# An octonion FFN and autocorrelation kernel: in the third hidden chunk of a group, the up unit is placed ahead of the down unit

## The reference, cut to what matters

```python
def _L0_ffn_ref(x, w_gate, w_up, w_down):
    ...
    xp = x.reshape(B, T, 8, D // 8)
    gate = oct_ternary_linear(xp, w_gate).reshape(B, T, -1)
    up = oct_ternary_linear(xp, w_up).reshape(B, T, -1)
    h = jax.nn.silu(gate) * up
    hp = h.reshape(B, T, 8, h.shape[-1] // 8)
    out = oct_ternary_linear(hp, w_down).reshape(B, T, D)
    return out

x = L0_attn_x
xn = _layernorm(x, axis=-1)
x = x + _L0_attn_ref(xn) + _L0_ffn_ref(xn, L0_ffn_w_gate, L0_ffn_w_up, L0_ffn_w_down)
```

## Time and profile before

| | |
|---|---|
| time, median of 3 runs | 612.71 us (612.17 to 613.39) |
| the profiled execution: time | 611.43 us |
| the profiled execution: span of its instructions | 609.6 us |
| TensorE busy | 575.1 us, 94% |
| VectorE busy | 506.1 us, 83% |
| GpSimd busy | 463.1 us, 76% |
| ScalarE busy | 356.4 us, 58% |
| granted TensorE clock, mean | 0.998 of full speed |

### The profile page before, as it was taken

One profiled execution on the slowest core, in us unless ns is written; L12 is line 12 of the kernel. 1 busy time (PEld: TensorE's weight loads), 2 busy tenths in 40 slices (PEclk: granted clock), 3 DMA queues, 4 the chain that ended last, 5 costly groups with the idle time before them and its releaser, 6 DMA issues.

```text
span 609.6 us, 16256 instructions
## 1 busy us (share of the span) xinstructions
PE 575.1 (94%) x6672; PEld 533.8 (88%) x6672; DVE 506.1 (83%) x1227; ACT 356.4 (58%) x499; POOL 463.1 (76%) x362
## 2 busy tenths in 40 slices
PE   0998999989999999999999999999999999999996
PEld 0898998878989999899989998899989998999896
DVE  1875799769899889989898989989888989967854
ACT  4767885755556645865567645774476545543540
POOL 2403919999778986999769977999779977987920
PEclk9999999999999999999999999999999999999999
DMA  9520003001030022101030013002030012002011
GB/s 226 135 72 1 1 1 140 2 1 57 16 139 2 2 72 65 76 2 70 2 140 1 9 65 126 15 2 71 2 139 1 35 38 70 2 2 70 2 71 70
DMA packets 10235, 30.65 MB, mean 50 GB/s; under 512 B 913, under 2 KB 4017, under 8 KB 10161
## 3 DMA queue, kind: packets, MB, share of 16 engines
q1 hardware_dynamic: 9200, 28.22, 13.9%
q10 hardware_dynamic: 960, 1.40, 1.0%
HBM read 21.23 MB, written 8.39 MB: 49 GB/s over the span
## 4 chain that ended last, share of the span: by engine, by line
POOL 53%; issue 30%; PE 12%; DVE 1%; DMA 1%; ACT 1%; POOLq 0%; SPq 0%; ACTq 0%
POOL hop L1299 15%; POOL hs L1293 10%; POOL hs L1294 10%; POOL hs L1289 9%; POOL hs L1288 6%; PE acc L462 5%; PE acc L393 4%; DMA xr<-in_x 1%; PE acc L372 1%; POOL r L1247 1%; POOL hop L1296 1%; PE acc L439 1%; PE acc L404 0%; PE acc L365 0%; ACT junk L584 0%
## 5 line engine op out<-in xcount | busy, mean ns | idle before, releaser
L462 PE MATMUL acc<-wd,hop 114*128 114x128 f16 (+1 forms) x2944 | 169.7, 219 | 1.0 <-POOL hop L1299 0.7
L462 PEld LDWEIGHTS acc<-wd,hop 114*128 114x128 f16 (+1 forms) x2944 | 166.6, 98 | 2.3 <-POOL hop L1299 0.9
L664 ACT ACTIVATE pk<-acc 114x512 f32<-114x512 f32 (+1 forms) x120 | 70.6, 589 | 70.4 <-PE acc L462 34.0
L1288 POOL TENSOR_TENSOR hs<-hx 114x512 f32<-114x512 f32 x47 | 60.3, 1283 | 66.8 <-DVE hx L1058 59.0
L1299 POOL TENSOR_TENSOR hop<-hs,hop 114x1024 f16<-114x1024 f32 x46 | 98.2, 2136 | 7.9 <-ACT hop L719 7.9
L1296 POOL TENSOR_TENSOR hop<-hx,hop 114x1024 f16<-114x1024 f32 x46 | 98.4, 2138 | 0.6 <-ACT hop L708 0.6
L372 PE MATMUL acc<-xop,wg 128*128 128x256 f16 x704 | 84.1, 273 | 4.5 <-DVE acc L1009 4.4
L708 ACT ACTIVATE hop<-hx 114x1024 f16<-114x1024 f32 x46 | 48.6, 1057 | 65.4 <-DVE hx L1058 65.4
L365 PE MATMUL acc<-xop,wg 128*128 128x256 f16 x704 | 84.2, 273 | 1.2 <-DVE hx L1058 1.1
L372 PE MATMUL acc<-xop,wu 128*128 128x256 f16 x704 | 84.1, 273 | 0.7
L365 PE MATMUL acc<-xop,wu 128*128 128x256 f16 x704 | 84.1, 273 | 0.7 <-DVE hx L1058 0.7
(11 more groups left out here) (156 smaller groups left out, 913.3 us busy)
## 6 DMA issues: line engine op xcount, KB each, us to landing
xr<-in_x SPq DMA_DIRECT2D x16, 512.0 KB, 4.6
zx<-in_x SPq DMA_DIRECT2D x16, 512.0 KB, 3.6
out_y<-zx SPq DMA_DIRECT2D x16, 512.0 KB, 3.0
hop<-in_w_down SPq DMA_DIRECT2D x1, 1364.0 KB, 19.1
hop<-in_w_gate ACTq DMA_DIRECT2D x1, 1152.0 KB
hop<-in_w_up SPq DMA_DIRECT2D x1, 1152.0 KB
hop<-in_w_gate ACTq DMA_DIRECT2D x1, 192.0 KB
hop<-in_w_up SPq DMA_DIRECT2D x1, 192.0 KB
```

Source lines behind the costliest of these rows:

```text
L462: last = nc.tensor.matmul(acc[:, bank[n], s // 2, at:at + P], operand(g, c, t, form, level), wd[0:WIDE[c], slot, c, :], start=which == 0 a ...
L664: nc.scalar.activation(pk[0:rows, q % 2, :, :], pair[:, :, T:2 * T], ACT.Copy, scale=XS if u[0] == "X" else 1.0).then_inc(copied, 1)
L1288: nc.gpsimd.tensor_tensor(hs[:, 4:8:2, :], h[:, 0:4:2, :], h[:, 1:4:2, :], ALU.add)
```

## The change

In groups 1 to 6 the unit N(g-1,1) moves from ahead of U(g,2,0) to behind it. On VectorE the output of an N unit moves behind the second sums when the step's own unit is a G (which is now so for N1, whose output falls into the step of G21, and for N(6,0) in the last group), and `x_sums_low` of X1 moves from the end of the step of G21 to the start of the step of U21. On ScalarE the rounding of the sums of U(g,1,0) stays in the step of N1 (`late` is 6), the rounding of U20 stays in the step of U21 (+4); the rounding of the sums of U20 is still six places behind its unit, which now is the step of G00 and was that of U00. The halves of `hop` are handed out as before (`written`).

```diff
@@ the order of the units
-            if c == 1 or c == 2 and g < G - 1:
-                units += [("N", g - 1, c - 1)]
+            if c == 1:
+                units += [("N", g - 1, 0)]
             units += [("U", g, c, 0)]
+            if c == 2 and g < G - 1:
+                units += [("N", g - 1, 1)]
@@ the halves of hop
-    for u in units:
+
+    def written(u):
+        return place[u] + (1.5 if u[0] == "U" and u[2:] == (2, 0) else 0)
+
+    for u in sorted((u for u in units if u[0] in "UN"), key=written):
@@ ScalarE's roundings
-            late = 6 if g == 0 or c == 2 else 4 if (c, Y, g) == (1, 0, G - 1) else 5
+            late = 6 if g == 0 or c == 2 else 4 if (c, Y, g) == (1, 0, G - 1) else 5 + (c == 1 and Y == 0)
             if (g, c) == (G - 1, NC - 1):
                 late = 4 + 3 * (1 - Y)
-            high_at[place[u] + 3] = u
+            high_at[place[u] + (4 if (c, Y) == (2, 0) and 1 <= g < G - 1 else 3)] = u
             round_at[place[u] + late] = u
@@ VectorE, one step
+                if n - 1 in x_sums and x_sums[n - 1][2] == 1:
+                    x_sums_low(x_sums[n - 1])
                 if u in quad_no:
                     first_adds(n, u)
...
-                if n >= OPEN + 2:
-                    v = units[n - 2]
-                    if v[0] == "N":
...
+                v = units[n - 2] if n >= OPEN + 2 else ("",)
+                if v[0] == "N" and kind == "G":
+
+                    second_adds(n, u)
+                if v[0] == "N":
...
-                if u in sums_no:
+                if u in sums_no and not (v[0] == "N" and kind == "G"):
                     second_adds(n, u)
...
-                if n in x_sums:
+                if n in x_sums and x_sums[n][2] == 0:
                     x_sums_low(x_sums[n])
```

More of the change, by code:

```diff
@@ L1137, in _ @@
                         split_last(v)
-                if n >= OPEN + 2:
-                    v = units[n - 2]
-                    if v[0] == "N":
[L1141 to L1150, removed]
-                if u in sums_no:
+                v = units[n - 2] if n >= OPEN + 2 else ("",)
+                if v[0] == "N" and kind == "G":
+                    second_adds(n, u)
+                if v[0] == "N":
+                    _, g, t = v
+                    pair = bank_pair(n - 2).rearrange("p b e -> p (b e)")
+                    res = zx[:, t, :]
+                    most = D - DB
+                    dve.wait_ge(term_mm, prod_no[v] + 1)
+                    dve.wait_ge(z_done, n_no[v] + 1)
+                    nc.vector.scalar_tensor_tensor(res[:, 0:most], pair[:, 0:most], osc[:, :], res[:, 0:most], ALU.mult, ALU.add)
+                    nc.vector.scalar_tensor_tensor(res[:, most:D], pair[:, most:D], nosc[:, :], res[:, most:D], ALU.mult, ALU.add).then_inc(out_done, 1)
+                elif v[0] == "F":
+                    least(v)
+                if u in sums_no and not (v[0] == "N" and kind == "G"):
                     second_adds(n, u)
```

## The result

The change makes the kernel slower: 626.13 us (median of 4 runs, 624.42 to 628.07) against 612.76 us of the kernel before beside it (612.17 to 613.39), a ratio of 1.0241 (1.0211 to 1.0271). The profiled execution took 626.38 us with a span of 624.6 us, 15.0 us more than before, where I had predicted 10.6. In a later batch on the chip the same kernel took 627.03 us (ratio 1.0251, 1.0219 to 1.0283).

A forecast was written before the change was run, and what follows sets the result against it. TensorE's matmuls (busy 94% of the span) plus its gaps bound the kernel. Five groups losing 2.2 us (+11.0) and 0.39 won in group 6 give +10.6 us: 612.71 becomes 623.3 us, own range 622 to 628, widened to 616 to 629.

The forecast's parts named there:

- VectorE's list: On VectorE, N1's output ends at 311.15 instead of 307.30 us, so F starts 0.8 us late.
- The loads: On SP, behind the store of N1's output, both row loads move 3.85 us; ScalarE's row sum waits 1.5 us.
- The rounding ahead of the copy: On ScalarE in G00's step, rounding of U20's sums (about 1.0 us) comes ahead of the copy VectorE needs for G00.
- my first rival: Row loads land soon enough; only the rounding delays the copy: G01 +0.4, U01 +0.5 us; 615 to 619 us; chance 0.13.
- The gap at G01: On TensorE, G01 is held by product U21 and starts at 321.55 instead of 319.48 us, +2.07 us.
- The loss of one group by its waits: On TensorE up to U01, 2.2 us in each of five groups, together +11.0 us.
- The end: Group 6: no row sum in F's step, G01 not held, 0.39 us won; later output of N(6,0) taken as nothing.
- The 0.39 us of gain: On TensorE, U21's terms start at 315.15 instead of 315.54 us: only 0.39 of 1.1 us won.
- The second: Faster: N1's output is out in time, F not held, both gaps go; 606 us, or 610.4; chance 0.08.
- the third: Slower still: late row sums drag next rows' statistics, or landings 5.5 us and more; from +16 us, 629 to 640; chance 0.09.
- the fourth: The forecast itself: loads land in 4.2 to 5.3 us, +9.6 to +15.5 us, 622 to 628 us; chance 0.68.

The follow-up runs named there:

- The kernel with the filler: Changed kernel plus 16 matmuls that nobody reads, in TensorE's pause ahead of G01 of groups 1 to 5; 622.83 us, ratio 1.0178.
- both causes away: Changed kernel with row loads issued ahead of the store and rounding of U20's sums back in the step of U00; 609.82 us, ratio 0.9982.
- the best kernel: Changed kernel with loads ahead of the store and rounding of U20's sums in F's step, between power and silu; 608.41 us, ratio 0.9945.

## Why the prediction was right, and where it was not

The sign, the places and the chain were as forecast, and 626.13 us lies 2.8 above the 623.3, inside the range. The share that the forecast missed is a mechanism that it did not hold, the clock. That it is no more than 2.8 us off is in part luck: by the spans it is 4.4 us off (15.0 instead of 10.6), but I had added 1.3 us for the median standing above the profiled execution, and this time it stood 0.25 below.

- **VectorE's list: right.** The output of N1 ends 9.36 us after X1's rounding starts (9.37 by the sum); the gap at L1009 is gone; F waits 0.68 us for the output, in all six, and starts 0.78 us later behind X1's transposes (12.32 instead of 11.54; 0.8 by the sum).
- **The loads: right.** They left SP at 317.38 behind the store, the first landed 4.3 us later (I took 4.4), and they held the row sum 1.15 to 1.74 us (1.5 by the sum), in five groups and not in the sixth. I took the landing of this very pair rather than the extremes; that of the other pairs differs by some tenths, and so do the gaps.
- **The rounding ahead of the copy: right.** With early loads G01 starts 0.39 us later (8.67 us behind F instead of 9.06, with F's own 0.78) and U01 0.5; my first rival had 0.4 and 0.5 for this. As a gap it shows as 0.64 us; with the late loads it adds 0.75.
- **The gap at G01: right.** Measured from F's start, G01 comes 0.9 to 1.5 us later than before (9.94 to 10.52 instead of 9.06), with F's own lateness 1.7 to 2.2, against 2.07.
- **The loss of one group by its waits: right.** F starts at 176.41, 247.59, 316.96, 387.68, 459.21 and 529.07 us, before at 175.73, 243.07, 310.42, 377.76, 445.37 and 512.70. Up to U01, and without the clock, the five groups lose 2.30, 1.79, 1.83, 2.37 and 2.28 us (F's lateness, G01's, and 0.13 at U01), 2.1 on average where I had 2.2.
- **N0's terms: not foreseen.** From F to F groups 2 and 5 lose 2.02 and 2.53 us, so 0.2 more each. It is a wait of N0's terms, whose transposes take 1.10 us (278.76 to 279.86) instead of 0.87, and it is there in these two groups alone. The statistics of the next rows are not late there: ScalarE's normalisation waits for nobody. What is longer is VectorE's first dot product, 1.80 us instead of 0.69:

```profile
272.45 1.80 DVE L926 SCALAR_TENSOR_TENSOR dj<-xr 128x512 f16<-128x512 f32 x1 [0.51 <-ACT xr L595]
```

- **The clock: missed.** In groups 1, 3 and 4 the way from F to F grew by 3.84, 3.38 and 3.92 us, 1.55 more than by the waits up to U01; that is the difference of the two blocks behind G01's start (5.17 us instead of 3.62). In these groups N0's terms don't wait, so against a group without a fall a fall costs 1.3 us net. Three falls are 4.65 us of the 15.0. In the second profile of the same kernel the four groups with a fall take 71.17 us on average, the one without 69.79: 1.4 us. What my sum lacked is a term: it priced the gap at G01 at its length, wrote that behind it nothing gives or takes, and left TensorE's clock out. The kernel with the filler shows it apart, 4.1 us less from F to F with more matmuls. The trace of before gave no warning: its groups hold no gap over 0.73 us, and behind its gap of 2.76 us in the opening the clock stayed up.
- **The end: a little better.** From F of group 6 to the end the kernel after takes 95.5 us instead of 96.9, and so does every kernel here with the new order (95.5 or 95.6). Of these 1.4 us, 0.8 make up for F's lateness, 0.41 are won at G01 (7.86 us behind F), which is the 0.39 of my sum, and 0.2 behind it, where I had counted the later output of N(6,0) as nothing.
- **Put together.** Up to the first F +0.7 (the openings of the eleven profiles end between 174.3 and 178.6 us, so this term is chance as much as F's lateness); five groups by their waits up to U01 10.6 (11.0 predicted); N0's terms 0.5 (0 predicted); clock 4.6 (0 predicted); the end -1.4. Sum 15.0.
- **The 0.39 us of gain: right, but only where nothing is next.** It was offset in this kernel, more than half given back with both causes away (0.16 left), and whole (0.41) once GpSimd had its half of `hop` in time. I had written that GpSimd gets its work earlier and no one waits for it. That is true of TensorE's waits by name; but with both causes away GpSimd's wait for the rounding reaches TensorE by way of the reciprocal root, ScalarE's normalisation and VectorE's dot products. In the kernel after this chain delays nothing at TensorE.
- **The rivals.** The loads did not land soon enough for the first. The second fell, since X1's rounding on VectorE is held by ScalarE's whatever the order, and cutting it in two gave nothing. Of the third neither part came: where TensorE waits at N0's terms, it is not for late statistics, and no first landing was 5.5 us or more. In the fourth the upper end is mis-added: 5.3 us to landing is 3.1 us a group and +15.1, not +15.5.

The Trainium skill's estimate of 3.2 us for a load of 512 KB ("DMA: Bandwidth & Descriptors", section on the anatomy of one DMA, given for the GpSimd-issued path) would have given +4.6 us; this pair, issued by SP, landed in 4.3 and 6.4 us, so the measurement decides against it here.

**What stays open.** Why the clock falls behind one gap and not behind another: it fell behind 1.94, 2.24, 2.27, 2.40, 2.41, 2.41 and 2.49 us and stayed behind 1.90, 2.34, 2.39 and 2.93. Length alone doesn't decide; nor does the place, since the gaps of group 5 (2.39 and 2.40 us) had a fall in one profile of the same kernel and none in the other, and the gap in the opening had one in some profiles only (below). Why VectorE's first dot product takes 0.69 us in one group and 1.80 in another, at the same distance from the transposes, is open too. And the wait of 0.68 us ahead of each F is left in the best kernel.

## What to carry to other kernels

When an output moves later in one engine's list, follow its signal through every queue behind it: here a store waited for it, and behind the store stood loads that have nothing to do with it. Issuing them ahead of the wait gave back 12 of the 13 to 15 us, the falls of the clock included. When TensorE gets gaps of about 2 us that it did not have, their length may not be the whole price (here 1.3 to 1.6 us more in seven of ten); look at the granted clock of the stretch behind them. A short operation that is only there for a slower reader belongs into a pause of its engine ahead of the hurried work, not at the place that a distance in steps gives it.

## What the runs showed of the hardware

- TensorE's granted clock fell to 0.5 (1.2 GHz) behind gaps of only 1.94 to 2.49 us in a kernel in which TensorE is busy 93% of the span, in 7 of the 10 such gaps of the two profiles of the kernel after. The two blocks behind took 5.17 us instead of 3.50. Behind gaps up to 1.5 us in these groups, in the profiles of five other kernels, it never fell, nor behind the one of 2.93 us. The opening has a gap of 2.76 us at 136 to 138 us in the kernel before and in all others; behind it the clock fell in 4 of 11 profiles. The Trainium skill ("TensorE: Matmul & The Clock Gate", Part 1, with its section on oscillation, and the table under "Why this matters for your kernels") tells of the two levels, and the trace agrees; by its rule for gaps in mid-kernel none this short should lower the clock, and there the trace does not agree.
- Cutting one VectorE instruction of 1024 elements in two made 1.37 us of busy time out of 1.23 (0.69 and 0.68), and the whole list up to `fold`, with the order that the cut forces, 0.33 us longer.
- A pair of row loads of 512 KB each, issued 0.4 us behind a store, landed in 4.3 and 6.4 us (before: 4.4 and 5.2).
- A VectorE dot product of 512 elements took 0.69 us in three groups of the kernel after and 1.80 us in the two others, the one behind it 1.57 in all.
